# Mixing stage of a long-convolution and mixture-of-experts layer: the last low part of each head on VectorE, the wait for list writes a step later, two tiles' lists a step in the last block

## The reference, cut to what matters

```
x = x + mix(ctx, ctx, layernorm(x), ssm_kernel, D)     # 16 x 512 x 1024
x = x + experts(layernorm(x))                          # router, 32 experts, 8 a token, one shared expert

mix(k, v, q, kernel, D), for each head h of 64 (8 channels each), all i, j of 8 x 8:
    kv[i,j] = k[i] * v[j]                               # k = v = ctx, so 36 pairs are enough
    y[i,j]  = causal convolution of kv[i,j] with kernel[h] over 1024 places, + D[h] * kv[i,j]
    out[j]  = sum over i of y[i,j] * q[i]

experts(t):
    scores = sigmoid(t @ router_w); groups of experts masked; the 8 best of the rest taken
    out    = sum over the 8 of weight * down(silu(gate) * up) + the shared expert
```

## Time and profile before

| | us |
|---|---|
| median of 3 runs | 14531.39 (14525.39 to 14533.43) |
| the profiled execution's own time | 14569.4 |
| span in the profile, first to last instruction | 14567.7 |
| TensorE busy | 14154.1 (97%) |
| VectorE busy | 5159.7 (35%) |
| POOL busy | 4261.2 (29%) |
| ScalarE busy | 3086.2 (21%) |
| mean granted TensorE clock | 0.986 of full speed |

### The profile page before, as it was taken

How to read it: one execution, slowest core, us unless ns; L and a number is a source line. 1 busy time by engine, 2 the same in 40 slices (tenths; PEclk the granted TensorE clock), 3 DMA queues, 4 the chain that set the end, 5 groups by cost and what they waited for, 6 DMA issues and landing times.

```text
span 14567.7 us, 197598 instructions
## 1 busy us (share of the span) xinstructions
PE 14154.1 (97%) x67488; PEld 11758.2 (81%) x67489; DVE 5159.7 (35%) x5698; ACT 3086.2 (21%) x4072; POOL 4261.2 (29%) x4357
## 2 busy tenths in 40 slices
PE   9989993999999999999999999999999999999999
PEld 7878783888888888888888888888888888888887
DVE  6877774122121222122212222313112112455544
ACT  4434441111111122112112222212111111111111
POOL 6778884111111111111111111111111112333333
PEclk9999996999999999999999999999999999999999
DMA  4555553122121232122212222313112112666666
GB/s 127 110 100 113 107 109 62 64 76 75 59 74 61 74 110 91 59 76 91 77 58 93 91 92 105 120 60 122 59 59 74 60 58 98 205 206 205 205 208 200
DMA packets 482743, 1491.03 MB, mean 102 GB/s; under 512 B 87745, under 2 KB 87873, under 8 KB 482450
## 3 DMA queue, kind: packets, MB, share of 16 engines
q0 software_dynamic: 286720, 890.00, 18.3%
q1 hardware_dynamic: 177938, 531.68, 13.4%
q10 hardware_dynamic: 17920, 67.12, 1.1%
HBM read 1083.97 MB, written 421.38 MB: 103 GB/s over the span
## 4 chain that ended last, share of the span: by engine, by line
PE 82%; DMA 0%; DVE 0%; issue 0%; ACT 0%; DVEq 0%; ACTq 0%; SPq 0%; POOLq 0%; POOL 0%
PE gps L1267 25%; PE ups L1267 25%; PE yps L1267 25%; PE xps L1274 4%; PE hps L1307 2%; DVE wlo L1195 0%; DMA raw<-in_L_ffn_w_up_dram 0%; ACT whi L1133 0%; DMA xg<-xnd,idx 0%; DVE yrow L1221 0%; DMA picked<-yd,gidx 0%; ACTq L1015 0%; DVEq L1015 0%; DVE xlo L1195 0%; DVE hlo L1195 0%
## 5 line engine op out<-in xcount | busy, mean ns | idle before, releaser
L1112 POOL DMA_INDIRECT yd<-yrow,yidx x544 | 575.6, 1058 | 7752.7 <-DVE yrow L1245 7752.7
L1231 DVE TENSOR_TENSOR hb<-hb,ups 128x512 f32<-128x512 f32 x672 | 462.1, 688 | 6196.5 <-ACT hb L1152 6196.5
L1267 PE MATMUL gps<-whi,xhi 128*128 128x512 f32 x5376 | 2157.2, 401 | 34.2 <-DVE wlo L1195 30.6
L1267 PE MATMUL ups<-whi,xlo 128*128 128x512 f32 x5376 | 2113.6, 393 | 0.0
L1267 PE MATMUL gps<-wlo,xhi 128*128 128x512 f32 x5376 | 2111.9, 393 | 0.0
L1267 PE MATMUL ups<-whi,xhi 128*128 128x512 f32 x5376 | 2111.3, 393 | 0.0
L1267 PE MATMUL gps<-whi,xlo 128*128 128x512 f32 x5376 | 2111.0, 393 | 0.0
L1267 PE MATMUL ups<-wlo,xhi 128*128 128x512 f32 x5376 | 2093.8, 389 | 0.0
L1152 ACT ACTIVATE hb<-gps 128x512 f32<-128x512 f32 x672 | 402.5, 599 | 6727.6 <-PE ups L1267 6702.7
L1267 PE MATMUL yps<-whi,hhi 128*128 128x512 f32 x5376 | 1726.3, 402 | 4.5 <-DVE hlo L1195 4.5
L1267 PE MATMUL yps<-wlo,hhi 128*128 128x512 f32 x5376 | 1674.2, 393 | 0.0
(11 more groups left out here) (166 smaller groups left out, 17985.3 us busy)
## 6 DMA issues: line engine op xcount, KB each, us to landing
raw<-in_L_ffn_w_gate_dram SPq DMA_DIRECT2D x128, 512.0 KB
raw<-in_L_ffn_w_up_dram SPq DMA_DIRECT2D x128, 512.0 KB
raw<-in_L_ffn_w_down_dram SPq DMA_DIRECT2D x64, 1024.0 KB
kT<-in_ctx_dram SPq DMA_DIRECT2D x64, 704.0 KB, 10.1
xin<-in_x_dram SPq DMA_DIRECT2D x64, 512.0 KB
thi<-kph SPq DMA_DIRECT2D x64, 512.0 KB, 7.0
tlo<-kpl SPq DMA_DIRECT2D x64, 512.0 KB, 8.8
xres<-in_x_dram SPq DMA_DIRECT2D x64, 512.0 KB
```

The costliest lines, as they stand in the source:

```text
L1112: pool.indirect_dma_start(out=yd, in_=yrow[i][:, :], in_offset=None, out_offset=bass.IndirectOffsetOnAxis(ap=yidx[i][:, 0:1], axis=0), bou ...
L1231: dve.tensor_tensor(hb[:, :], hb[:, :], ups[:, :], ALU.mult).then_inc(h_done, 1)
L1267: ins = pe.matmul(ps, rows, w[:, chunk, i * 512:(i + 1) * 512], start=first and n == 0, stop=last_one and n == 2)
```

## The change

Three things change in the mixing stage.

1. The fourth low part of each head (group 3) moves from POOL's kv_lower(3) to a new function last_kv_lower on VectorE, which stands behind the residual add of the same step and has a semaphore of its own, kv_low_last. kv_low now counts three a head. POOL's products 1 of the next step, which write the same buffer kv[1], wait for kv_low_last, and so do TensorE's conv(3) and conv_opposite of the head a step later.
2. POOL's wait for the block's list writes and the release of place move from the end of step u = 6 to the end of step u = 7, behind kv_lower(2), as free_place. VectorE's assign in the same step u = 7 waits for this release.
3. In block 8 each of the four steps issues the lists of two tiles; after the walk only free_place is left.

```diff
--- before.py
+++ after.py
@@ -284,7 +284,8 @@
         mean_out, var_out, sqrt_out = sem("mean_out"), sem("var_out"), sem("sqrt_out")
         scale_in, normed, scale_out, normed2 = (sem("scale_in"), sem("normed"), sem("scale_out"),
                                                 sem("normed2"))
-        kv_built, kv_high, kv_low = sem("kv_built"), sem("kv_high"), sem("kv_low")
+        kv_built, kv_high = sem("kv_built"), sem("kv_high")
+        kv_low, kv_low_last = sem("kv_low"), sem("kv_low_last")
         xin_mm, q_copied = sem("xin_mm"), sem("q_copied")
         y_mm, y4_mm, y_used, y4_used = sem("y_mm"), sem("y4_mm"), sem("y_used"), sem("y4_used")
         reduced = sem("reduced")
@@ -359,7 +360,10 @@
                 n, kk = s.n(KVS), kT[s.slot(KVS)]
                 if q == 0:
                     pool.wait_ge(k_ld[s.slot(KVS)], 16 * (s.half(KVS) + 1))
-                wait(pool, kv_low, GROUPS * n + q - 1)
+                if q == 1:
+                    wait(pool, kv_low_last, n)
+                else:
+                    wait(pool, kv_low, (GROUPS - 1) * n + (0 if q == 0 else q - 1))
                 row = XC * B
                 pool.tensor_tensor(kv[q % 2][:, :, 0:MAIN].rearrange("p r (d c) -> p r d c", d=LAGS),
                                    view(kk, 2 * q, 0, [[row, 2], [0, LAGS], [1, P]]),
@@ -385,24 +389,28 @@
                 kv_lower(s, 1)
                 pair_products(s, 3)
                 kv_lower(s, 2)
-                kv_lower(s, 3)
-                if s.u < 7 and routes(s, s.u, 2):
+                if isinstance(s.block, int) and s.block == BLOCKS - 1:
+                    list_tokens(s.block - 2, (2 * s.u, 2 * s.u + 1))
+                elif s.u < 7 and routes(s, s.u, 2):
                     list_tokens(s.block - 2, ((0,), (1,), (2,), (3,), (4,), (5,), (6, 7))[s.u])
+                elif routes(s, 7, 2):
+                    free_place(s.block - 2)
 
             def list_tokens(r, tiles):
                 pool.wait_ge(placed, r + 1)
                 settle(pool, pool_turns)
                 for t in tiles:
                     list_tile(pool, lists, toki, place, t, listed)
-                if RB - 1 in tiles:
-                    pool.wait_ge(listed, 16 * RB * K * (r + 1))
-                    pool.sem_inc(place_free, 1)
+
+            def free_place(r):
+                pool.wait_ge(listed, 16 * RB * K * (r + 1))
+                pool.sem_inc(place_free, 1)
 
             pool.sem_inc(place_free, 1)
             pool.wait_ge(lists_st, 32)
             pool.wait_ge(kpad_st, 32)
             walk(pool, step)
-            list_tokens(NTILE // RB - 2, (4, 5, 6, 7))
+            free_place(NTILE // RB - 2)
 
         @block.scalar
         def _(act):
@@ -532,6 +540,15 @@
                                   mybir.AxisListType.XY, ALU.add).then_inc(reduced, 1)
                 dve.wait_ge(reduced, GROUPS * n + g + 1)
 
+            def last_kv_lower(s):
+
+                if not s.on(KVS):
+                    return
+                n, i = s.n(KVS), s.slot(KVS)
+                dve.wait_ge(kv_high, GROUPS * (n + 1))
+                dve.tensor_tensor(klo[i][:, 6:8, :], kv[1][:, :, :], khi[i][:, 6:8, :].bitcast(F32), ALU.subtract)\
+                    .then_inc(kv_low_last, 1)
+
             def step(s):
                 times_queries(s, TAIL, 3)
                 opposite_pairs(s, TAIL, 2)
@@ -560,6 +577,7 @@
                     dve.wait_ge(r_ld, 16 * (n + 1))
                     dve.wait_ge(out_mm, n + 1)
                     dve.tensor_tensor(xr[:, :], xr[:, :], ps[:, :], ALU.add).then_inc(out_added, 1)
+                last_kv_lower(s)
                 opposite_pairs(s, CONV, 1)
                 sum_terms(s, CONV, 1)
                 if s.on(OUT):
@@ -693,7 +711,10 @@
                 n, sl = s.n(CONV), s.slot(CONV)
                 if g == 0:
                     pe.wait_ge(t_ld[sl], 32 * (s.half(CONV) + 1))
-                pe.wait_ge(kv_low, GROUPS * n + g + 1)
+                if g < GROUPS - 1:
+                    pe.wait_ge(kv_low, (GROUPS - 1) * n + g + 1)
+                else:
+                    pe.wait_ge(kv_low_last, n + 1)
                 wait(pe, y_used, GROUPS * n + g - 1)
                 passes = ((thi, khi), (thi, klo), (tlo, khi))
                 for lb in (2 * g, 2 * g + 1):
@@ -709,7 +730,8 @@
                 if not s.on(CONV):
                     return
                 n, sl = s.n(CONV), s.slot(CONV)
-                pe.wait_ge(kv_low, GROUPS * (n + 1))
+                pe.wait_ge(kv_low, (GROUPS - 1) * (n + 1))
+                pe.wait_ge(kv_low_last, n + 1)
                 wait(pe, y4_used, GROUPS * n)
                 passes = ((thi, khi), (thi, klo), (tlo, khi))
                 for d in range(LB):
```

## The result

The changed kernel takes 14396.39 us (median of 4 runs, 14394.22 to 14404.77), the kernel before 14529.4 us beside it (4 runs, 14525.39 to 14533.43): a ratio of 0.991, interval 0.9892 to 0.9927, 133 us faster. The forecast was 14449 us, 82 us faster, with a range that ended at 14400. The direction held, and so did the mechanism of the moved wait; the gain was 51 us larger. Some 27 of these lie in the moved wait, and some 24 in what the moved low part brings.

The account below looks back on a forecast made before the run. TensorE was taken to bound ordinary steps, with VectorE setting the pace from line 740 to conv(1) in blocks 2 to 5. Terms 70 - 12 + 22 + 2 = 82 us gained: median 14531.4 to 14449 us, range 14400 to 14500.

Parts of the forecast that it names:

- The wait for list writes, a step later: POOL's six waits in blocks 2 to 7 leave its order; TensorE gains 70 us, bounds 60.3 and 107.9.
- the 38.0 us between the profiled execution and the median: Unprofiled runs are shorter; if TensorE is less short of instructions there, more of the 107.9 us is real.
- Rival 1: TensorE is not short of instructions without the profiler: the wait gains the whole 107.9 us, 14411 us; chance 0.20.
- The last low part on VectorE: The subtraction, 1.36 us, is on the path in nine steps: 12 us lost, bounds 0 and 36.
- The lock between VectorE and POOL: Two-input VectorE subtraction may lock with POOL's SBUF instructions, up to 36 us lost; 12 kept, since POOL would be waiting.
- The assignment: VectorE's assignment overlaps POOL less: 3.7 us for each of six, 22 us gained; bounds 0 and 6.8 each.
- place_free: VectorE's wait inside the assignment before rewriting list positions, costed at 0; 18 us were each landing over by 3 us.
- rival 2: The list-write wait only changes its place, to VectorE at place_free: gain shrinks to 22 us, 14509 us; chance 0.11.
- Two tiles a step: Last block's 64 writes start one low part sooner, 2.7 us; 2 us gained in step 65, bounds 0 and 3.
- rival 3: VectorE, late with the subtraction, bounds every step: 56 us slower, 14587 us; chance 0.05.

Follow-up runs that it names:

- before_again: The kernel before, unchanged, run and profiled once more; 14527.75 us beside 14525.7 us of the same kernel, ratio 1.0.
- third_buffer: The changed kernel with a third kv buffer for group 3, so POOL's products 1 no longer wait for VectorE's subtraction; 14507.76 us, ratio to the kernel before 0.9955.
- after_again: The changed kernel, unaltered, run again on a chip with the shortage of instructions; 14466.66 us beside 14573.63 us of the kernel before, ratio 0.9929.
- low_on_vector_only: The kernel before with only the fourth low part moved to VectorE, the wait for list writes left in place; 14474.94 us, ratio 0.9966.

## What the prediction had right, and the steps that failed

**The wait for list writes, a step later (70 taken, bounds 60.3 and 107.9).** This term of the sum is the step that failed. Alone it measured 97 us; the twelve steps in which it was looked for are 96.6 us shorter. The value was taken "nearer to what was seen", and what was seen came from an execution in which TensorE was late in those steps because it was short of instructions. For such a chip the terms for these steps are good: 84 us forecast, 87.9 found, though the whole gain there was 107 and not 82. The measured median lies with the executions in which TensorE arrives on time, stands 127 us, and gets nearly all of POOL's time back. The prediction had the sign in its hand, the 38.0 us between the profiled execution and the median, named as a possible meaning that TensorE arrives earlier in them, and still carried the difference over from one to the other. That carrying over is the error; had the 70 been 107.9, the forecast would have been 14411, 15 us from the result.

**Rival 1** is that case by its size. Its cause stands corrected: the shortage does not come from the profiler (before_again is profiled and free of it), and by their times unprofiled runs on other chips have it too (14564 to 14587 us).

**The last low part on VectorE (-12; bounds 0 and -36).** With the assignment's term this is the second place where the sum failed: all its other terms make 12 us (-12 + 22 + 2), and 133 - 97 = 36 us were measured. The cost of the instruction was right: median 1.352 us for the forecast 1.36, and 9.5 us on the path for 12. But part of the gain lay elsewhere in the sum (16.1 us of POOL's earlier arrival within the bound of 107.9, 22 us of the assignment), and with its own terms only, the edit looked like a loss. Alone it gains 51 us; on top of the moved wait 32 to 35 (from 14428.7 to 14396.4 and 14394.0), for which the terms make 16 + 22 - 12 = 26. The 1.50 us of waiting for the high part, which goes with it (in five of six blocks of before_again, 7.4 us in sum), stood in the earlier trace rows and was not counted. And the two steps with choose_groups, put at 1.36 us lost each, became 4.2 us shorter each. The prediction puts them in blocks 1 and 6; the later one is in block 7. The two parts alone make 97 + 51 = 148 and together 133, since both shorten the same step.

**The lock between VectorE and POOL.** The upper end of 36 us came from the lengthened rows. The choice of the low value, because POOL would stand waiting for this very subtraction, was right: third_buffer lets POOL go on, and the subtraction takes up to 6.53 us, 39.7 us more in sum. The rule of the Trainium skill, page "SBUF — State Buffer", section on its two sides, agrees with these rows in that the two engines' instructions exclude each other; here the subtraction that took 6.20 us was passed by more than one instruction of POOL's.

**The assignment (22).** The case it was taken from, block 1 "with POOL quiet", is misread: POOL works through the whole of it in the first trace of before.

```profile
471.80 2.67 POOL L377 TENSOR_TENSOR klo<-kv,khi 128x1152 fp32r<-128x1152 f32 x1 [0.56 <-ACT khi L415]
474.43 2.44 POOL L364 TENSOR_TENSOR kv<-kT 128x1024 f32<-128x1024 f32 x1
476.82 2.50 POOL L367 TENSOR_TENSOR kv<-kT 128x128 f32<-128x128 f32 x1
479.29 4.33 POOL L364 TENSOR_TENSOR kv<-kT 128x1024 f32<-128x1024 f32 x1
```

So the 22 was a guess between its bounds. The assignment fell from 94.6 (before_again) to 81.4 us over six blocks, 13, in the trace of after; in after_again by some 31 against the first trace. Its place is where the gain now ends: TensorE waits 39.5 us in the six u = 0 steps for VectorE, and these steps grew by 17 us. Splitting the assignment takes it back, 42.5 us in these steps.

**place_free (0).** No idleness before line 676. Landings are on record only for the last 64 writes, behind the walk: a median of 14.4 us from the issue and a maximum of 18.9 in after, 16.1 and 19.8 in before_again. The "about 15 us" of rival 2 is near them, but the first trace of before has no landing on record; its six waits, 91.8 us, have a mean of 15.3. Nothing speaks for rival 2.

**Two tiles a step (2).** 0 within the measurement. Step 65 did not grow in the traces without the shortage (32.2 us); with it, 95.3 to 107.6 us stand against 100.9.

**VectorE as the bound of every step (rival 3).** Ordinary steps remain at 32.6 us; of the steps looked at, it bounds those with the assignment.

In front of the prediction the walk is said to stand at line 136; it stands at 142.

## What to carry to other kernels

Where a profiled execution is longer than the median of the others, find out first which stage holds the difference, and price a wait by both pictures: with an engine late for another reason, as TensorE was here, the idleness that it shows is a lower bound and not an estimate. When work is moved between VectorE and GpSimd, count what the moved instruction makes the other engine wait for, too: a wait that keeps GpSimd out of SBUF while VectorE works may be worth more than the instruction costs, and an extra buffer that removes it may lose, as it did here. After a gain of this size look at which engine ends the wait in the next step; here half an assignment, moved by one step, gave 26 us more on a chip without the shortage and 6 on one with it.

## What the runs showed of the hardware

The shortage of instructions belongs neither to the program nor to the profiler: step 65 takes 32.2 us in every trace on two of the chips used and 95 to 108 us on a third, for kernels that do the same there, with one matmul in 2.8 us (0.37 us of it busy) as long as GpSimd issues list writes. On a fourth, where the kernel before is as slow as on the third, the step takes 32.2 us with the writes held back. Whether it is the chip, and what differs between them, stays open. The Trainium skill, page "Runtime: NRT & Kernel Launch", section "Instruction fetch mechanics", says that each engine fetches its instructions through a DMA queue of its own and that the cost is mostly hidden. The 2.43 us of "issue" before each matmul could be such a fetch showing; whether they are, and whether the list writes delay that queue, no run shows.

While GpSimd makes its products and subtractions, small VectorE operations can be long as well: 64 numbers a row took 2.21 us with GpSimd at work (before_again) and 0.27 without (low_on_vector_only), and a 128x1152 subtraction took 1.35 to 6.53 us (third_buffer).
